# A two-layer decoder on one core: products with the values in 64-row halves, and 512-wide units with shared tails

## What is computed

```python
x = _layernorm(x + _L0_attn_ref(x, ...))                    # causal self-attention, 2048 x 2048
x = _layernorm(x + _L0_xattn_ref(x, ctx, ctx, mask, ...))   # cross attention to 1601 rows, with a mask
x = _layernorm(x + _L0_ffn_ref(x, ...))
x = _layernorm(x + _L1_attn_ref(x, ...))                    # causal self-attention and an MLP
x = _layernorm(x + _L1_xattn_ref(x, ctx, ctx, ...))         # cross attention to 1601 rows, no mask
x = _layernorm(x + _L1_ffn_ref(x, ...))                     # mixture of experts
# each attention:
scores = scale * einsum('bhqd,bhkd->bhqk', q, k)
attn = softmax(scores)
out = einsum('bhqk,bhkd->bhqd', attn, v)
```

## Time and profile before

| | us |
|---|---|
| median of 3 runs | 3052.56 (3050.74 to 3059.14) |
| the profiled execution | 3052.74, span 3051.0 |
| PE busy | 2817.6 (92% of the span) |
| VectorE busy | 2171.2 (71%) |
| ScalarE busy | 1824.3 (60%) |
| causal attention of layer 0, first to last head moved out | 171.0 to 543.5 |
| masked cross attention, the same | 690.3 to 1313.3 |
| causal attention of layer 1, the same | 1501.0 to 1864.2 |
| unmasked cross attention, the same | 2125.9 to 2680.6 |

### The profile page before, as it was taken

The page is one execution under the profiler, slowest core; times in us unless marked ns, Lnnn a source line. Parts: engine busy times, 40 slices in busy tenths (PEclk is TensorE's granted clock), DMA queues, the critical chain, the costliest instruction groups (busy, mean ns, idle before and its releaser), DMA issues. The chain is left out here.

```text
span 3051.0 us, 93944 instructions
## 1 busy us (share of the span) xinstructions
PE 2817.6 (92%) x39186; PEld 1046.2 (34%) x39187; DVE 2171.2 (71%) x6062; ACT 1824.3 (60%) x2158; POOL 542.7 (18%) x760
## 2 busy tenths in 40 slices
PE   4999999999999999967999998999999999899997
PEld 2522222522222222233222224652222222256664
DVE  7688986587878887565899993158888888652114
ACT  2388878436666666734588886234777777831222
POOL 0188870110000000001222113111000000002330
PEclk7899999979999999978899999997999999999999
DMA  3345541301110001102111112020111111111112
GB/s 98 111 130 131 135 111 35 118 18 25 25 26 25 17 24 26 36 20 76 33 47 43 42 45 83 1 74 23 39 52 52 52 53 32 35 58 62 44 43 86
DMA packets 120407, 166.79 MB, mean 55 GB/s; under 512 B 38227, under 2 KB 89310, under 8 KB 119984
## 3 DMA queue, kind: packets, MB, share of 16 engines
q1 hardware_dynamic: 102192, 117.21, 14.3%
q0 software_dynamic: 12320, 43.02, 4.6%
q10 hardware_dynamic: 5472, 0.56, 0.2%
HBM read 126.51 MB, written 26.72 MB: 50 GB/s over the span
## 5 line engine op out<-in xcount | busy, mean ns | idle before, releaser
L737 DVE TENSOR_REDUCE mpart<-ps 128x1 f32<-128x512 f32 (+2 forms) x1792 | 1014.2, 616 | 149.2 <-PE ps L548 148.1
L548 PE MATMUL ps<-stack 48*32 48x401 f16 (+5 forms) x13312 | 987.9, 355 | 55.3 <-DVE mpart L737 25.3
L475 ACT ACTIVATE xT<-ps,exp_scale 128x1024 f32<-128x1024 f32 (+3 forms) x800 | 794.6, 1028 | 284.6 <-PE ps L569 137.5
L475 ACT ACTIVATE cn<-ps,exp_scale 128x1024 f32<-128x1024 f32 (+4 forms) x800 | 743.1, 959 | 233.6 <-PE ps L569 119.7
L569 PE MATMUL ps<-stack 50*32 50x512 f16 (+3 forms) x11648 | 744.4, 377 | 56.2 <-ACT xT L475 42.3
L548 PEld LDWEIGHTS ps<-stack 48*32 48x32 f16 x13312 | 293.3, 91 | 1056.6 <-DVE mpart L737 562.8
L733 DVE CUSTOM_DVE_ANT_0 scrap<-ps,arena 128x401 bf16<-128x401 f32 (+1 forms) x1024 | 534.3, 574 | 128.0 <-PE ps L548 128.0
L609 PE MATMUL ps<-xT,vall 128*17 128x512 f32 (+4 forms) x3648 | 422.5, 524 | 2.2 <-POOL xT L434 1.4
L609 PE MATMUL ps<-cn,vall 128*17 128x512 f32 (+3 forms) x3392 | 412.9, 508 | 1.0 <-ACT cn L475 1.0
L569 PEld LDWEIGHTS ps<-stack 50*32 50x32 f16 x11648 | 194.6, 91 | 209.2 <-ACT xT L475 110.5
L727 DVE CUSTOM_DVE_ANT_0 scrap<-ps,scrap 128x128 bf16<-128x128 f32 (+3 forms) x512 | 247.6, 485 | 19.7 <-PE ps L548 15.1
(11 more groups left out here) (281 smaller groups left out, 2510.9 us busy)
## 6 DMA issues: line engine op xcount, KB each, us to landing
stack<-q_parts SPq DMA_DIRECT2D x384, 64.0 KB, 2.6
stack<-k_parts SPq DMA_DIRECT2D x192, 64.0 KB, 2.9
wbuf<-in_maskT POOLq DMA_DIRECT2D x24, 512.0 KB, 4.7
arena<-in_moe_w SPq DMA_DIRECT2D x19, 512.0 KB, 4.4
stack<-k_parts SPq DMA_DIRECT2D x192, 50.0 KB, 2.3
stack<-sums_inverse SPq DMA_DIRECT2D x16, 512.0 KB, 5.6
parts<-osb SPq DMA_DIRECT2D x240, 32.0 KB
wbuf<-in_mask POOLq DMA_DIRECT2D x16, 401.0 KB, 4.0
```

What stands on the lines that cost most here:

```text
L475: nc.scalar.activation(e.prob[tile % P_SLOTS][0:rows, half * HALF + first:(half + 1) * HALF], S_PS(g)[0:rows, first:HALF], ACT.Exp, scale= ...
L548: last = nc.tensor.matmul(bank[quarter(j), 0:w], qs[b][rows, t * P + 32 * j:t * P + 32 * j + 32], ks[b][rows, a:a + w], start=True, stop=True)
L737: nc.vector.tensor_reduce(dst, src, AX, ALU.max).then_inc(unit_used, 1)
```

## The change

The change touches `attention_phase` alone.

1. In the three unmasked attentions a product is done in two halves of rows: `upper_keys` takes keys 0 to 63 of the tile (rows 0 to 63 of TensorE), `lower_keys` keys 64 to 127. The upper half is issued in the slot that ends the tile (one slot later where `select` is set: `lag = 1`), the lower half one slot after the upper. Both add to the same bank, and each waits on a semaphore until the other before it has finished: `lower_keys` of a tile for its `upper_keys` (`pv_half`), `upper_keys` of a tile for the `lower_keys` of the tile before (`pv_done`).
2. Units that follow `lower_keys` go to rows 0 to 63, and units that follow `upper_keys` to rows 64 to 127, instead of by turns.
3. In the unmasked cross attention units are 512 keys wide, three to a tile of queries, and the last 65 keys of four tiles of queries share one unit (16 matmuls of 65 columns, one reduction of 4 x 65): 52 units a head instead of 64.
4. With `select`, the copy out stands behind the second exponential of the next head instead of the first. The products' number of PE instructions doubles; the masked attention's loop is written in another form with the same order.

```diff
+    wide = not causal and not masked
     for t in range(NT):
         cut = tiles((t + 1) * P, CH) if causal else tiles(keys, -(-keys // -(-keys // CH)))
-        units += [(t, i, a, w, causal and a + w == (t + 1) * P) for i, (a, w) in enumerate(cut)]
+        if wide and t % 4 == 0:
+            units += [(t + j, i, a, CH, False, 1) for j in range(4) for i, (a, _) in enumerate(tiles(keys, CH)[:-1])]
+            units.append((t, keys // CH, keys // CH * CH, keys % CH, False, 4))
+        elif not wide:
+            units += [(t, i, a, w, causal and a + w == (t + 1) * P, 1) for i, (a, w) in enumerate(cut)]
...
+        lag = 1 if select else 0
...
-                        if n == 0 and h:
+                        if n == lag and h:
                             copy_out(h - 1)
...
-                    bank, first = e.ps[:, g % M_BANKS, :], g % 2 * ROWS
+                    bank, first = e.ps[:, g % M_BANKS, :], (g % 2 if group is None else group) * ROWS
                     rows = slice(first, first + KQ)
-                    for j in range(4):
-                        last = nc.tensor.matmul(bank[quarter(j), 0:w], qs[b][rows, t * P + 32 * j:t * P + 32 * j + 32],
-                                                ks[b][rows, a:a + w], start=True, stop=True)
+                    for i in range(count):
+                        for j in range(4):
+                            at = (t + i) * P + 32 * j
+                            last = nc.tensor.matmul(bank[quarter(j), i * w:i * w + w], qs[b][rows, at:at + 32],
+                                                    ks[b][rows, a:a + w], start=True, stop=True)
...
+                def product(h, kt, some, closes):
+
+                    tile, rows = h * nk + kt, k_tiles[kt][1]
+                    some = slice(some.start, min(some.stop, rows))
                     weights = e.prob[tile % P_SLOTS].rearrange("p (b j q) -> p b j q", j=4, q=P)
                     for j in range(4):
                         b0 = max(0, -(-(kt - j) // 4)) if causal else 0
                         if b0 == 4:
                             continue
...
+                        end = closes and kt == (12 + j if causal else nk - 1)
+                        last = nc.tensor.matmul(O_PS[quarter(j, HD + 1), b0 * P:CH], e.values[some, kt, h, :],
+                                                weights[some, b0:4, j, :], start=(kt == 0 and some.start == 0), stop=end)
+                    return last
...
+                def upper_keys(g):
+
+                    h, kt = g // ns, slots[g % ns][0]
+                    pe.wait_ge(exp_done, g + 1)
+                    pe.wait_ge(pv_done, h * nk + kt)
+                    opened(h, kt)
+                    product(h, kt, slice(0, ROWS), False).then_inc(pv_half, 1)
+
+                def lower_keys(g):
+
+                    h, kt = g // ns, slots[g % ns][0]
+                    pe.wait_ge(pv_half, h * nk + kt + 1)
+                    product(h, kt, slice(ROWS, P), True).then_inc(pv_done, 1)
...
+                        closing, opening = ends_tile(g - lag - 1), ends_tile(g - lag)
+                        if not closing:
+                            middle = 0
+                        elif not opening:
+                            middle = len(now)
+                        if closing:
+                            lower_keys(g - lag - 1)
+                        for u in now[:middle]:
+                            unit(turned, u, 0)
+                        if opening:
+                            upper_keys(g - lag)
+                        for u in now[middle:]:
+                            unit(turned, u, 1)
...
+                    elif count > 1:
+                        several = e.ps[:, g % M_BANKS, 0:count * w].rearrange("p (t n) -> p t n", n=w)
+                        nc.vector.tensor_reduce(e.mpart[h % 2][:, t:t + count, piece], several, AX, ALU.max).then_inc(unit_used, 1)
```

More of the change, by code:

```diff
@@ L534, in value_part, with unit @@
                         part.then_inc(front_made, 1)
-                def unit(h, u):
-                    t, piece, a, w, diagonal = units[u]
+                def unit(h, u, group=None):
+                    t, piece, a, w, diagonal, count = units[u]
                     g, b = h * nu + u, h % 3
@@ L660, in _, with ends_tile @@
                         mask_scores(0, n)
-                for h in range(H):
-                    for n in range(ns):
-                        if n + 2 < ns:
-                            scores(h, n + 2)
-                        elif h + 1 < H:
-                            scores(h + 1, n + 2 - ns)
-                        turned = h + (1 if n <= turn else 2)
-                        now = range(before[n], share[n]) if turned < H else range(0)
-                        middle = -(-len(now) // 2)
+                def ends_tile(g):
+                    return 0 <= g < H * ns and slots[g % ns][5]
@@ L670, in _ @@
+                for g in range(H * ns):
+                    h, n = divmod(g, ns)
+                    if g + 2 < H * ns:
+                        scores(*divmod(g + 2, ns))
+                    turned = h + (1 if n <= turn else 2)
+                    now = range(before[n], share[n]) if turned < H else range(0)
+                    middle = -(-len(now) // 2)
+                    if masked:
                         for u in now[:middle]:
                             unit(turned, u)
-                        if masked and h * ns + n + 2 < H * ns:
-                            mask_scores(h + (n + 2) // ns, (n + 2) % ns)
@@ L674, in _ @@
-                        if slots[n][5]:
-                            product(h, n)
+                        if g + 2 < H * ns:
+                            mask_scores(*divmod(g + 2, ns))
+                        if ends_tile(g):
+                            whole(g)
                         for u in now[middle:]:
                             unit(turned, u)
+                    else:
+                        closing, opening = ends_tile(g - lag - 1), ends_tile(g - lag)
[11 more added lines that the diff above has]
+                            unit(turned, u, 1)
@@ L678, in _ @@
+                if not masked:
+                    for g in range(H * ns, H * ns + lag + 1):
+                        if ends_tile(g - lag - 1):
+                            lower_keys(g - lag - 1)
+                        if ends_tile(g - lag):
+                            upper_keys(g - lag)
                 pe.wait_ge(o_weights_in, 16 * NC)
```

19 lines of the change are left out of this document (9 added, 10 removed).

## The result

The changed kernel takes 3307.84 us (median of 4 runs, 3285.01 to 3349.47), the kernel before 3055.85 beside it: a ratio of 1.08, 95% interval 1.0741 to 1.086. It is slower by 8%; 3028 was forecast. The profiled execution has a span of 3305.8 us, 254.8 more than before.

What follows compares the result with a forecast made beforehand. VectorE was taken as close to full in the causal attentions, and bound in a loop with three banks and the undivided product in the cross attention. 3052.7 - 70 (cross) + 46 (causal) = 3028 us; this case 3000 to 3045, range 2968 to 3092.

Steps and rivals of the forecast that it cites:

- about 1.1 us for the lower clock, as today: Unmasked cross attention: lower clock costs 1.1 us of a forecast 32.9 us head, unchanged by the edit.
- 1 us a head either way: Clock falling more often in causal tails, or no longer in the cross attention, would shift the forecast by this much.
- held by ScalarE: nothing: Last cross attention heads: they have no units and ScalarE holds them, so the change there is zero.
- Net +1.75 a head: Causal attention of layer 1: net loss from half products and later copy, 15 heads, +26 us.
- +2.15 less 1.1 of cover: Causal tiles 8 to 15: chained halves add 2.15 us a head; covered waits return 0.9 and 0.2.
- +0.7: Causal heads: later copy out, from 0.45 us of half product and a displaced exponential.
- the causal tail costs double: Rival, chance 0.16: each chain wait also delays the unit behind it; 3.5 us a head, 30 heads, +105, total 3088.
- 30.6 + 1.2: Cross attention head: 30.6 us of VectorE work plus 1.2 of new wait for the delayed copy out.
- The wide units alone are worth 0.8 us a head: Cross attention: VectorE's work falls from 31.4 to 30.6 us a head with 512-wide units.
- the loop of banks and product: Cross attention before: VectorE, three banks and the 0.99 us undivided product form a loop, 2.78 us a tile.
- The rival at 0.06: Program order holds on PE: about 0.1 us more a slot; cross -34, causal +46 and +48, total 3113.
- the last rival: Chance 0.05: halves do not overlap; 3.1 us a tile against 2.78, some 4 us a causal head, total 3200.

Runs made afterwards that it cites:

- e3: The kernel before, with each product in the unmasked attentions taking only keys 0 to 63 of a tile, the other keys left out: 3307.18 us.
- e5: The changed kernel plus eight unused 48-row matmuls beside half products in slots without units, all three unmasked attentions: 3293.12 us.
- e8: The kernel before with both parts of the change in the unmasked cross attention alone, plus spare matmuls in its last head: 3031.33 us, ratio 0.9923.
- e6: The changed kernel with each unit of the causal attentions' tiles 8 to 15 done twice into the same bank: 3467.49 us.
- e10: The changed kernel with both half products of the causal attentions' tiles 8 to 15 over all 128 rows, same waits, keys counted twice: 3466.89 us.
- e11: e1 with the unmasked cross attention's product in two halves of queries, 256 columns each, all 128 rows: 3069.21 us, ratio 1.0025.
- e4: The changed kernel with whole products in tiles 8 to 15 of the causal attentions, halves kept elsewhere: 3138.73 us.
- e1: The changed kernel with whole products everywhere and the copy out where it was; only the cross attention's 512-wide units stay: 2998.88 us, ratio 0.9825.
- e7: The changed kernel with a slot's units issued ahead of its half product instead of behind it: 3585.93 us.

## Why the prediction was wrong

**The step that failed** is the clock. The text priced it as a bystander: "about 1.1 us for the lower clock, as today", and, should it fall more often in the causal tails, "1 us a head either way". It took the clock to be the same when a product uses 64 rows instead of 128. e3 shows that it is not: with 64-row products and nothing else the clock of whole attentions falls. In the changed kernel the last heads take 106 us more (47.9 + 31.4 + 26.7), which the forecast had at nothing ("held by ScalarE: nothing"). Where the spare matmuls held the clock, they gave back the larger part of that: 25.3 of 47.9 in causal 0 (e5) and 21.3 of 26.7 in the cross attention (e8); in causal 1, where they held it for a part of the time, 3.7 of 31.4 (e5). What they did not give back is the half products that follow one another, or the spare matmuls themselves. In each causal head the clock costs about 1.4 us: one low stretch of 3.4 us, priced by cross heads of 36.1 and 34.7 us with two and one of them. Over 26 heads that is 36 us. No rival had it. An estimate for the whole program: 625 us at the lower clock instead of 292 in the two profiled executions, at 1.4 us for each 3.4, make 137 of the 255 us. What beside the rows brings the clock down stays open: in e6, e10 and e11 it fell where no expectation had it.

**The chain in the causal tail** was the right mechanism and mis-sized. "Net +1.75 a head" measured +6.3 (30.7 - 24.4), of which 1.4 is the clock, so 4.9. The waits themselves are as forecast (0.70 for 0.68). By e4, 3.0 of the 4.9 lie in the tail (30.7 - 1.4 - 26.35), where the text had +2.15 less 1.1 of cover, and 1.9 in tiles 0 to 7 and at the copy (26.35 - 24.4), where it had +0.7. In the tail the cover did not come: VectorE waits there for results held behind half products, as the row at 1724.74 shows, and ScalarE for its buffers. How the 1.9 splits was not tried. The rival "the causal tail costs double", at 3.5 us a head, came nearest and named the waiting units.

**The cross attention** in its middle went as written: halves side by side with units, VectorE full, 1.2 us a slot. The gain was 25.6 us for 14 heads instead of 69. At full clock the sum had 31.8 us a head (30.6 + 1.2), measured 33.4; for the clock it had 1.1, measured 2.4 (35.8 - 33.4). And the gain is not the halves': e1 has it without them. The sentence "The wide units alone are worth 0.8 us a head" was the second error of size: 36.35 - 33.3 = 3.0 at full clock, since a wider unit also lengthens what three banks hold. I had named the loop of banks and product, and then priced the wide units by VectorE's work alone.

**The order of results.** I weighed the Trainium skill's rule (TensorE: Matmul & The Clock Gate, "The mechanism"), that matmuls start and end in program order, against the earlier trace rows and gave it 0.06. The rule and I each had half of it. Starts are not in program order across halves: the unit of 1724.04 starts ahead of the second pass, at 1724.22, of the half product issued before it. But the unit's release at 1724.74 instead of 1724.49 fits ends in order. The rival at 0.06 had just this ("A unit is then done no earlier than the half product ahead of it"), and its 46 + 48 for the causal heads was nearer to the 120 below than the forecast's 46. e7 left it open beyond this reading of the trace. The price of the last rival, 3200, is a slip: by its own terms, 0.3 us for each of 13 tiles in 14 heads and 4 us for 30, it comes to some 3230.

**The count.** Halves at full clock in the causal heads +120 (73.9 + 82.0 - 36), clock in them +36, last heads +106, cross attention -26, the rest +19: 255 us. The +18.5 was not taken apart; it lies mostly ahead of causal 0's first copy, where TensorE was at the lower level for 37.5 us from 134.4 on, against 17.1 us from 133.8 on before.

## What to carry to other kernels

A busy PE is not a warm one: before cutting a matmul to fewer rows so that it fits beside another, ask what keeps the clock up in every stretch, above all where the other has run out, and price each such stretch at 1.2 GHz as well. Two parts that wait for each other through semaphores follow one another at the full length of each (0.70 us for one of 0.63 here), and what is issued behind them can wait too. When an engine starves behind a block of another, first count how long the buffers between them last; a bigger piece per buffer gave 1.8% here, with nothing else changed.

## What the runs showed of the hardware that was not expected

- Products of 64 rows instead of 128, in the same number, took causal 1 from a granted clock of 1.00 to 0.50 for all of its 466 us, with PE 97% busy.
- Rows are not all: products of 128 rows and 256 columns instead of 512, twice as many, took the cross attention from 31 to 154 us of low time (e11 against e1, one profile of each).
- A clock once lost can stay lost for many heads: 46.7 us or 30.8 for the same work in e6, 51.4 or 31.8 in e10. The changed kernel's time went with its granted clock: 3285.01 us at 0.915, 3307.59 at 0.905.
- Added work can speed a kernel up: the spare matmuls took the last cross head from 54.8 to 33.5 us and the kernel from 3052.32 to 3031.33 (e8). Added work of the same kind in another place did not (e6).
- A 32-bit half product in 64 rows and a 16-bit unit in the other 64 run side by side without slowing each other: 2419.86 to 2420.30, 0.44 us from first to second pass, with a unit that began at 2420.01. In a whole product before, with no unit beside it, the second pass also came 0.44 us behind the first (2383.17 and 2383.61).
